# An audio tower on one core: chunks of the last stage staggered, softmax shares split into two single-pass products, softplus by chunk, means on GpSimd

## What is computed

```python
h = tok(x)                                   # patch embedding, layer norm
h = h + ssm(_layernorm(h), ...)              # 16 states per channel
h = h + moe(_layernorm(h), ...)              # 6 experts, one per token
h = h + _L1_attn_ref(_layernorm(h), ...)     # window of 7, 16 heads
h = h + _L1_ffn_ref(_layernorm(h), ...)      # 6 experts, all of them, weighted by sequence
```

```python
delta = jnp.minimum(jax.nn.softplus(x_ssm @ delta_W + delta_b), 0.5)
B_cont = 0.5 * (B_cont - jnp.mean(B_cont, axis=(0, 1), keepdims=True))
...
attn = jax.nn.softmax(attn, axis=-1)                    # 7 offsets x 16 heads
out = jnp.einsum('bhlk,bhlkd->bhld', attn, vg)
out = out.transpose(0, 2, 1, 3).reshape(B, L, C)
return out @ proj_w.T + proj_b
...
h = jax.nn.gelu(jnp.einsum('bsd,edf->ebsf', x, W1) + b1[:, None, None, :], approximate=False)
out_e = jnp.einsum('ebsf,efd->ebsd', h, W2) + b2[:, None, None, :]
return jnp.einsum('be,ebsd->bsd', expert_weights, out_e)
```

## Time and profile before

| | us |
|---|---|
| median of 3 runs | 953.21 |
| the runs | 950.11, 953.21, 1652.1 |
| the profiled execution, its own time | 950.27 |
| its span, first to last instruction | 948.3 |
| busy in the span: TensorE, VectorE, ScalarE, GpSimd | 643.1, 663.2, 487.5, 261.9 |
| mean granted TensorE clock | 0.835 |

### The profile page before, as it was taken

How to read it: one execution, slowest core, us unless ns; L and a number is a source line. 1 busy time by engine, 2 the same in 40 slices (tenths; PEclk the granted TensorE clock), 3 DMA queues, 4 the chain that set the end, 5 groups by cost and what they waited for, 6 DMA issues and landing times.

```text
span 948.3 us, 11034 instructions
## 1 busy us (share of the span) xinstructions
PE 643.1 (68%) x2992; PEld 473.6 (50%) x2993; DVE 663.2 (70%) x1458; ACT 487.5 (51%) x691; POOL 261.9 (28%) x266
## 2 busy tenths in 40 slices
PE   6984353745647527576650799357898898988986
PEld 3552253745546527553450477224555655655564
DVE  1977279999999999996862344266767677667651
ACT  1234699888989888831330233115353463443632
POOL 0443100000010001001487144231525426345242
PEclk9985677877768777698755799688999999999998
DMA  5300333553345434514211121200000000000000
GB/s 179 118 12 0 130 113 75 93 105 80 64 90 110 76 75 72 99 20 169 96 30 33 37 59 53 62 14 0 1 9 1 8 9 1 9 1 9 8 2 16
DMA packets 22519, 50.63 MB, mean 53 GB/s; under 512 B 4610, under 2 KB 14955, under 8 KB 22128
## 3 DMA queue, kind: packets, MB, share of 16 engines
q0 software_dynamic: 6752, 24.53, 13.2%
q1 hardware_dynamic: 15728, 25.64, 8.6%
HBM read 24.13 MB, written 10.10 MB: 36 GB/s over the span
## 4 chain that ended last, share of the span: by engine, by line
PE 39%; DVE 29%; issue 11%; ACT 10%; POOL 5%; POOLq 2%; DMA 2%; ACTq 1%; DVEq 0%; SPq 0%
PE psum L1715 5%; DVE s_R L1049 5%; DVE s_R L1059 5%; PE psum L1477 4%; DVE s_R L1054 4%; PE psum L1779 3%; PE psum L1644 3%; PE psum L1707 3%; PE psum L1657 2%; ACT s_R L879 2%; DVE s_R L1028 2%; POOLq L178 2%; POOL x_sorted L619 2%; DVE s_stat L203 2%; DVE s_xs L237 2%
## 5 line engine op out<-in xcount | busy, mean ns | idle before, releaser
L1538 PE MATMUL psum<-s_xn_lo,s_split_hi 128*128 128x368 f32 x256 | 101.3, 396 | 147.6 <-ACT s_R L783 99.2
L1538 PEld LDWEIGHTS psum<-s_xn_lo,s_split_hi 128*128 128x128 f32 x256 | 59.3, 232 | 153.2 <-ACT s_R L783 101.7
L1715 PE MATMUL psum<-s_R 128*128 128x368 f32 (+1 forms) x288 | 101.5, 473 | 0.0
L1054 DVE TENSOR_TENSOR_SCAN s_R<-s_R 128x2944 f32<-128x2944 f32 x16 | 100.7, 6291 | 0.6
L879 ACT ACTIVATE s_R<-psum,s_cols 128x368 f32<-128x368 f32 x96 | 52.2, 569 | 91.4 <-PE psum L1709 91.4
L1539 PE MATMUL psum<-s_xn_hi,s_split_lo 128*128 128x368 f32 x256 | 97.4, 381 | 0.0
L1540 PE MATMUL psum<-s_xn_hi,s_split_hi 128*128 128x368 f32 x256 | 96.6, 377 | 0.0
L604 POOL DMA_DIRECT2D s_xnfm<-s_R x14 | 17.1, 1219 | 271.2 <-DVEq L1063 271.2
L665 POOL TENSOR_TENSOR s_R<-s_R 128x368 f32<-128x368 f32 x48 | 45.4, 946 | 108.6 <-DVE s_R L1333 105.6
L1715 PEld LDWEIGHTS psum<-s_R 128*128 128x128 f32 (+1 forms) x288 | 53.0, 189 | 27.6
L1707 PE MATMUL psum<-s_xn_lo,s_split_hi 128*128 128x368 f32 x144 | 61.0, 424 | 7.1 <-ACT s_R L879 5.6
(11 more groups left out here) (219 smaller groups left out, 1506.0 us busy)
## 6 DMA issues: line engine op xcount, KB each, us to landing
s_xnfm<-s_R POOLq DMA_DIRECT2D x14, 1472.0 KB, 10.6
s_R<-in_xg SPq DMA_DIRECT2D x8, 744.0 KB, 4.2
x_sorted<-in_x_init SPq DMA_DIRECT2D x1, 5082.0 KB, 19.7
s_R<-in_w SPq DMA_DIRECT2D x2, 1536.0 KB, 9.5
s_wBC<-in_wBC SPq DMA_DIRECT2D x8, 256.0 KB, 2.9
s_R<-x_sorted SPq DMA_DIRECT2D x28, 66.0 KB, 1.8
s_R<-y_rows SPq DMA_DIRECT2D x8, 184.0 KB
out<-s_R SPq DMA_DIRECT2D x8, 184.0 KB
```

The costliest lines, as they stand in the source:

```text
L1054: dve.tensor_tensor_scan(bufB[:, u], ra[:, u], bufB[:, u], 0.0, ALU.mult, ALU.add).then_inc(ra_free, 1)
L1538: pe.matmul(bank(c), w_hi[:, s, u, k, :], xn_lo[:, a:b], start=True, stop=False)
L1715: ins = pe.matmul(bank((2, 4)[e % 2]), w, fh[0:kk, e % 3, j], start=(j == 0), stop=(j == FT - 1))
```

## The change

1. The barrier between stages 1 and 2 goes. ScalarE takes Exp and Ln per chunk, `softplus(i - 1)`, between `norm_second` and the copies of the next pair; a table set for both is asked for at the start; VectorE caps the argument instead of taking the minimum at the end. The first `wBC` is loaded with the first loads, and its split moves into stage 1. The first state's B and C go before the second state's Exp, Tanh and Exp.
2. The mean of B moves from VectorE (L1045, L1047) to GpSimd (`mean_of`, three small operations and a new wait of `drive`). GpSimd waits for the accumulation before it issues the next, not after. `weights_lo` goes ahead of `read_out`, and `read_out` no longer waits for itself.
3. Stage 5 has 10 turns. In turn `c`: attention of chunk `c`; projection, residual, norm and router of `c - 1`; the first 18 items of `FFN` for `c - 1`; the last 18 for `c - 2`. All four streams are reordered. One pair of items in `FFN` changes place.
4. The shares are split in `P_hi` (ScalarE, from PSUM) and `P_lo` (VectorE, PSUM less `P_hi`), and each offset's spread is two single-pass products instead of one fp32 product. `xn_hi`, `xn_lo` of the last stage hold two chunks only, which makes the room.

```diff
         def stage_end(eng, k):
             eng.drain().then_inc(stage_done, 1)
-            eng.wait_ge(stage_done, 4 * k)
+            eng.wait_ge(stage_done, 4 * (k - 1))
...
# list FFN
-               + [(1, 5, j) for j in range(FT)] + [(2, e, j) for e in (4, 5) for j in range(FT)])
+               + [(1, 5, 0), (1, 5, 1)] + [(2, 4, j) for j in range(FT)] + [(1, 5, 2)]
+               + [(2, 5, j) for j in range(FT)])
...
# GpSimd, stage 2
-            stage_end(pool, 1)
+            pool.wait_ge(x_split, NCH)
+            pool.wait_ge(delta_mm, NCH)
...
+            def add_state(n, u, first=False):
+                wait_apart(pool, prod_ready, n + 3)
+                if not first:
+                    wait_apart(pool, Y_added, 16 * n)
                 pool.dma_start(Y[:, :], bufC[:, u], accum_op=ALU.add, max_dma_last_dim=TOK // 2 * 4)\
                     .then_inc(Y_added, 16)
-                pool.wait_ge(Y_added, 16 * n + 16)
+            def mean_of(n, u):
+                wait_apart(pool, bc_free, NH + (n * 2 + 1) * NH)
+                wait_apart(pool, th_free, n + 1)
+                step.add(pool.tensor_tensor(part[:, u, 0:2], part[:, u, 0:2], part[:, u, 2:4], ALU.add))
+                step.wait()
+                step.add(pool.tensor_tensor(mean[:, u:u + 1], part[:, u, 0:1], part[:, u, 1:2], ALU.add))
+                step.wait(True)
+                pool.tensor_scalar(mean[:, u:u + 1], mean[:, u:u + 1], 1.0 / TOK, 0.0, ALU.mult, ALU.add)\
+                    .then_inc(mean_ready, 1)
+            mean_of(0, 0)
+            mean_of(1, 1)
+            add_state(0, 0, True)
+            add_state(1, 1)
+            for i in step.loop(NPAIR - 2, 2 * 2):
+                for u in range(2):
+                    mean_of(i * 2 + 2 + u, u)
+                for u in range(2):
+                    add_state(i * 2 + 2 + u, u)
+            mean_of(NS - 2, 0)
+            mean_of(NS - 1, 1)
...
# ScalarE, stages 1 and 2
+            act.preload_act_table_set("natural_log_exp_and_others")
...
+            def softplus(i):
+                for u in range(2):
+                    c = i * 2 + u
+                    d = dl[:, 1 + c * CT:1 + c * CT + CT]
+                    act.wait_ge(delta_read, 2 + c + 1)
+                    act.activation(d, d, ACT.Exp).then_inc(delta_act, 1)
+                    act.wait_ge(delta_act, 2 * c + 1)
+                    act.activation(d, d, ACT.Ln, bias=1.0, scale=1.0).then_inc(delta_act, 1)
+            bias_copy(0)
+            weights_hi(0, 0)
+            for i in range(NP):
+                if i + 1 < NP:
+                    bias_copy(i + 1)
+                normed_twice(i)
+                if i:
+                    softplus(i - 1)
+                norms_fm(i)
+            softplus(NP - 1)
+            load_table(ACT.Tanh, 0)
+            tanh(0, 0)
+            exp_minus(0)
+            exp_plus(0, 0)
+            silus(0, (0,), True)
+            exp_plus(1, 1)
+            tanh(1, 1)
+            exp_minus(1)
             weights_hi(1, 1)
+            silus(0, (1,), True)
...
# VectorE, stage 2
             def drive(n, u):
-                dve.wait_ge(bc_free, NH + (n * 2 + 1) * NH)
-                step.add(dve.reduce_sum(mean[:, u:u + 1], part[:, u, :], axis=AX))
-                step.wait()
-                step.add(dve.tensor_scalar(mean[:, u:u + 1], mean[:, u:u + 1], 1.0 / TOK, None, ALU.mult))
-                step.wait()
+                dve.wait_ge(ea_free, n + 2)
+                dve.wait_ge(mean_ready, n + 1)
...
# ScalarE, VectorE and TensorE, stage 5
+                act.activation(P_hi[:, c % 2], bank(3, OH), ACT.Copy).then_inc(P_hi_ready, 1)
+                dve.tensor_tensor(P_lo[:, c % 2], bank(3, OH), P_hi[:, c % 2].bitcast(f32), ALU.subtract)\
+                    .then_inc(P_fm_ready, 1)
-                        pe.matmul(bank(6 + o % 2), spread[:, o, :], P_fm[:, u], start=True, stop=True).then_inc(pb_mm, 1)
+                pe.matmul(bank(6 + o % 2), spread_r[:, o, :], P_lo[:, c % 2], start=True, stop=False)
+                pe.matmul(bank(6 + o % 2), spread_r[:, o, :], P_hi[:, c % 2], start=False, stop=True).then_inc(pb_mm, 1)
```

More of the change, by code:

```diff
@@ new lines, in _ @@
+            step.add(pool.memset(euler, math.e))
+            step.wait()
+            rstd_e(0)
+            for c in range(NCH + 2):
+                add_expert(c - 3, 5)
+                if c + 1 < NCH:
+                    rstd_e(c + 1)
+                add_expert(c - 2, 0)
+                add_expert(c - 2, 1)
+                if 1 <= c <= NCH:
+                    rstd_f(c - 1)
+                add_expert(c - 2, 2)
+                add_expert(c - 2, 3)
+                if c < NCH:
+                    projection_bias(c)
+                add_expert(c - 2, 4)
+                if c < NCH:
+                    weighted_sum(c, lambda: second_share(c - 1) if c else None)
+                elif c == NCH:
+                    second_share(c - 1)
@@ L912, in act_chunk @@
[L912 to L924 removed]
+                gelus(c - 2, 18, 21)
@@ L1080, in pair @@
                     decay(n + 3, 1)
-            dve.sem_inc(w_split, 1)
-            weights_lo(0, 0)
             injection(0, 0)
             decay(0, 0)
+            drive(0, 0)
+            recur(0, 0)
+            read_out(0, 0)
             decay(1, 1)
             injection(1, 1)
-            pair(0, 1)
-            for i in step.loop(NPAIR // 2 - 1, 2 * (2 * 2 + 2 * 3)):
+            weights_lo(1, 1)
+            drive(1, 1)
+            recur(1, 1)
+            injection(2, 0)
+            decay(2, 0)
+            read_out(1, 1)
+            injection(3, 1)
+            decay(3, 1)
+            for i in step.loop(NPAIR // 2 - 1, 2 * 2 * 2):
                 pair(i * 2 + 1, 0)
@@ new lines, in offset @@
+            def offset(c, o):
+                dve.wait_ge(pb_mm, c * K + o + 1)
+                if o >= 3:
+                    dve.wait_ge(pv_add, c * (K - 1) + o - 2)
+                dst_t = pv[:, c % 2] if o == 0 else pv_t[:, o % 2]
+                for dst, a, b in windowed(c % 2, o, bank(6 + o % 2), 2, dst_t):
+                    ins = dve.tensor_tensor(dst, a, b, ALU.mult)
+                ins.then_inc(pb_free, 1)
+            first_experts(0)
+            normed_e(0)
+            for c in range(NCH + 2):
+                f, att = c - 1, c < NCH
+                tail = 0 <= f < NCH
+                if 0 <= f - 1:
+                    expert_weights(f - 1)
+                weigh_expert(f - 1, 0)
+                weigh_expert(f - 1, 1)
+                if c + 1 < NCH:
+                    first_experts(c + 1)
+                if att:
+                    score_products(c)
+                if c == 0:
@@ new lines, in _ @@
+                weigh_expert(f - 1, 3)
+                if tail:
+                    normed_f(f)
+                if att:
+                    shares(c)
+                if tail:
+                    split_stream(f)
+                if att:
+                    shares_rest(c)
+                if tail:
+                    stream_sums(f)
+                weigh_expert(f - 1, 4)
+                for o in range(K):
+                    if att:
+                        offset(c, o)
+                    if o == 1 and c + 1 < NCH:
+                        normed_e(c + 1)
+                    if o == 2 and tail:
+                        router_largest(f)
+                    if o == 3:
+                        weigh_expert(f - 1, 5)
+                    if o == 4 and tail:
+                        router_second(f)
+                    if o == 5 and tail:
+                        router_weights(f)
@@ L1524, in _, with states @@
             delta(NP - 1)
-            stage_end(pe, 1)
-            def states(i, s):
+            def states(i, s, first=False):
                 for u in range(2):
@@ new lines, in project, with quarter @@
+            def project(c):
+                if c + 1 < NCH:
+                    pe.wait_ge(qkv_ready, (c + 1) * 3 + 1)
+                else:
+                    pe.wait_ge(pb_free, NCH * K)
+                pe.wait_ge(pv_add, (c + 1) * (K - 1))
+                for j in range(CB):
+                    ins = pe.matmul(bank_tm(6)[:, j, :], pv[:, c % 2, j * L:(j + 1) * L], w_proj, start=True, stop=True)
+                ins.then_inc(proj_mm, 1)
+            def quarter(q):
+                return psum[32 * q:min(32 * q + 32, OH), 3, 0:CT]
```

677 lines of the change are left out of this document (323 added, 354 removed).

## The result

| | us |
|---|---|
| median after, 4 runs | 919.6 (917.96, 919.01, 920.19, 920.49) |
| median before, beside them | 952.86 (lowest 950.11) |
| ratio | 0.967, 95% interval 0.965 to 0.969 |
| the profiled execution, its own time | 919.01 |
| its span | 917.2 |

The kernel is 33 us faster, inside the range and on the forecast side. The forecast was 912; it came out 7.6 slower. Three executions lie far above the rest and count in no ratio: 1652.1 and 987.8 of the kernel before, and 2055.6 of one experiment.

What follows compares the result with a forecast made beforehand. VectorE bounds the scan loop; in the last stage no engine is full, TensorE nearest. Stage 2 gives 12.5 us and the last stage 26, together 38.5 off 950.3: 912, own range 898 to 924, wider range 886 to 934.

Steps and rivals of the forecast that it cites:

- start of the last stage: Stage 5 begins 12.5 us earlier, from both parts of stage 2 together.
- to the first expert product of chunk 7: Tail of the last stage, from the last sixth offset: 17.3 us, where it was 10.8.
- Between stages 1 and 2: First drive at 116.4 instead of 133.0, 16.6 us earlier; 10 of it taken as kept at state 4.
- The tables rival: Between stages 1 and 2, each chunk's Exp and Ln load tables, 10 us back: 922 in total; chance 0.08.
- The pairs: Pairs of states in stage 2: 0.5 us less a pair, over 5.5 pairs from state 4 on, 2.7.
- The ring: One last-stage turn's circle through TensorE and VectorE: 32.6 us, plus 2.2 of blocking, period 34.8.
- The blocking of 2.2: Last stage: VectorE loses 2.2 us a turn to four GpSimd sums, 0.8 before the scores, 0.9 the shares, 0.5 later offsets.
- Six turns at 34.8: 209: Last stage: six turns after the second take 34.8 us each, 209 in all.
- The spreads: Last stage: seven spreads as two single-pass products each instead of one fp32 product, 2.0 us less TensorE work a turn.
- Full cover: Rival: VectorE and GpSimd rarely meet, last-stage period 32, means cost nothing, the start keeps 12: 888 us; chance 0.22.
- Hand-overs: Rival: TensorE and VectorE wait in turn, last-stage period 37.5, tail 50.5, stage 2 gains 8: 934 us; chance 0.17.
- The stalled scan: Rival: in stage 2 drive waits for GpSimd's means, up to 4.1 us a state: 980 us, slower; chance 0.03.

Runs made afterwards that it cites:

- the kernel with the front alone: The kernel before with only the edits of stages 1 and 2: 935.5 us, ratio 0.983.
- their experiment: The changed kernel with the means back on VectorE, sum and scale inside drive: 920.1 us, ratio 0.967.
- the moved bias addition: The changed kernel with GpSimd's addition of the projection bias moved behind expert sum 4: 906.3 us, ratio 0.953.
- the new order: The changed kernel with the shares of c ahead of the norm of f, transposes and copies alike: 900.8 us, ratio 0.948.
- the kernel with the earlier norm: The changed kernel with VectorE's norm of chunk c + 1 behind offset 0 instead of offset 1: 910.2 us, ratio 0.957.
- the experiment: The changed kernel with one fp32 product per spread instead of two single-pass products, without P_lo: 926.2 us, ratio 0.973.
- two moves of lines: The changed kernel with the shares ahead of the norm of f and the norm of c + 1 behind offset 0: 897.3 us, ratio 0.943.
- the front of before: The kernel before with only the edits of the last stage: 937.2 us, ratio 0.984.
- both moves: The changed kernel with the bias addition behind expert sum 4 and the shares ahead of the norm of f: 901.6 us, ratio 0.949.

## Why the prediction was right, and where it was off

The sum was 922.2 - 12.5 = 909.7 of span, measured 917.2; the 7.5 between them, step by step:

| step | forecast | measured |
|---|---|---|
| start of the last stage, against 611.5 | 12.5 earlier | 13.4 earlier; 13.0 to 16.7 in the other profiles with the front's edits |
| end of its first turn (sixth offset read) | 622.9 | 621.7 |
| second turn, to the next sixth offset | 29 | 29.4 |
| six turns | 209, 34.8 each | 215.1, 35.9 each; four dips in them |
| to the first expert product of chunk 7 | 17.3 | 18.1 |
| from there to the end | 31.5 | 32.9 |

That the start of the last stage came within 0.9 of the forecast is luck: three misses cancel there, the late start, a term of the pairs that was too small, and 2.5 lost behind the pairs (all below).

*Between stages 1 and 2: right.* Forecast 116.4 for the first `drive`; 114.6 to 115.8 in the profiles of all kernels with these edits, 118.62 in the one with the late start. At state 4 the kernel with the front alone is 9.0 ahead (10 forecast). The tables rival fell: ScalarE's timeline of the changed kernel has no load between those at 0.72 and 103.36, so none between the small activations. The 0 taken for it had no row of the kernel before behind it, only the name that the edit asks for.

```profile
100.68 0.51 ACT L767 ACTIVATE s_R<-s_R 128x368 f32<-128x368 f32 x1 [0.72 <-DVE s_R L1049]
101.23 0.51 ACT L769 ACTIVATE s_R<-s_R 128x368 f32<-128x368 f32 x1
...
103.36 1.28 ACT L745 ACT_TABLE_LOAD   x1
```

*The pairs: mis-sized.* The term was 0.5 a pair, "over 5.5 pairs from state 4 on: 2.7". It is 38.34 less 36.88, 1.5 a pair; from 9.0 ahead at state 4 the kernel with the front alone gets to 16.6 ahead at the last state. I had counted 0.5 and 0.76 to 1.3 and taken most of it back for the blocking. The means are worth 0.3 (their experiment), so 1.2 comes from the other edits of stage 2. No run takes these apart; what the timelines show gone are VectorE's waits around `read_out` and `weights_lo` (0.33, 0.26 and 0.30 in the pair of the earlier trace rows), which I had put at 0.5. (The two terms of stage 2, 10 and 2.7, make 12.7, not the 12.5 used.) Of these 16.6 (397.87 against 414.46), 2.5 are lost again before the last stage; where, no run settles.

*The ring: right in its length.* Forecast 32.6 and 2.2 of blocking, 34.8; measured 34.9 wherever the clock is full. From the turn that begins at 728.8 on: transposes to scores' end 12.3 (forecast 11.9 + 0.8), to the first spread 11.1 (10.6 + 0.9), to the transposes 11.5 (10.1 + 0.5). So two parts came 0.4 short of the forecast and the third 0.9 over, of which 0.37 is the wait for an offset; that the sum is off by 0.1 only is partly luck. The blocking of 2.2 is not where I put it either. The products of q and k take 3.07 in both kernels, so the expert sums cost nothing there; the norm of f loses 1.65 instead of 0.9, since the bias addition, which I had left out, falls on it as well. That the blocking on the shares stands on the ring is shown by the moved bias addition (34.9 to 33.9) and by the new order (33.1).

*The failed step: "Six turns at 34.8: 209".* It priced none of the six at a lower clock, as the five turns before from 686.36 on had none. Six turns took 6.1 longer, and of the 7.5 missed this is most: the six have four dips, and the turns without one take 34.9. One turn, with 37.1, is even above the 37 at which the prediction calls itself wrong. My ring named the idle time ahead of the first spread ("with some 1.7 left idle"; it is 1.8 for the shares and 0.5 for `P_lo`), but not that the clock can fall behind it. It falls at this place in every full turn with a dip of every profile. The five kernels in which this wait is at most 0.5 from the third turn on have no dip until the last 8 us; all that have one wait 0.9 or longer for the shares. So, by these profiles, the wait is part of the cause, but not all of it: the kernel with the earlier norm keeps it and four of its turns have no dip, and the kernel before waits 1.02 at this place and has none. Waits of 1.81 and 0.49 stand ahead of the fall at 782.5, and the same two also stand in turns at 1.00. By what mechanism the clock falls no run shows.

*The spreads* were priced at 2.0 a turn by their work; the experiment gives 0.8 by whole executions and 1.2 by the profiles, with a change in the dips in it.

*The rivals.* Full cover (888) needed a ring of 32: two moves of lines come near it, 32.6 and 897, so the bound was sound and this order just does not reach it. (For it, I had put most of TensorE's 3.9 idle round the softmax; the longest of these waits, 1.25, is for GpSimd's last sum, and 1.02 is for the shares.) Hand-overs (934) had turns of 37.5; the only one near it, 37.1, has a dip, which is another mechanism. The stalled scan fell: the waits for the means are 0.7 a pair, not 2.3 a state.

What stays open: why a given turn dips while the next, with the same idle 1.8, does not. It does not look like chance: two kernels that differ in stage 2 alone have the same pattern (turns of 35.44, 36.45, 34.88, 37.16, and with the means moved 35.48, 36.47, 34.87, 37.16), and the pattern is another with the front of before (four turns with a dip, and the last at 1.00). But each kernel has one profile only, so whether its pattern repeats is not shown.

## What to carry to other kernels

When an order of work is computed from durations at the full clock, look at TensorE's longest wait in the new ring as well: it is paid a second time if products behind it run at the lower clock (1.6 or 2.3 a turn here). Here the kernel before, with 3.9 idle in a turn but no wait above 1.25, had no dip, and the shorter ring with one wait of 1.8 had some. Beside a chain that GpSimd's sums can block, put VectorE's most urgent instructions first and the blocked ones behind them (900.8 against 919.6 here); moving the sum only helps if it does not land on the next such instruction (with both moves TensorE waited 1.08 for an offset instead of 0.39). Moving small operations to GpSimd from a VectorE that never rests saves little, since each of them can wait for a whole long instruction (3.00 instead of 0.2; 0.3 gained a pair here, for 0.76 of work moved).

## What the runs showed of the hardware

- More work, less time: 12 transposes added a turn gave 913.3 instead of 919.6 (3.3 of it seen in the last stage), and products of constants in the first turns 894.5 instead of 897.3.
- The clock fell to half (0.51 from 782.5 to 789.5) in a loop in which TensorE was busy for 32 of 34.9 us: for 4 us or for 7, always behind the same wait, at a price of 1.6 or 2.3 a turn.
- Who came second waited. VectorE's seven products of q and k, back to back, take 3.07, and GpSimd's normalization beside them (L226 at 766.62, 0.19 in the median) takes 3.24; but between the four short instructions of VectorE's norm of f GpSimd's sum of 1.00 gets in, and the norm takes 1.75 instead of 1.08, and 2.73 with the bias addition of 1.26 beside it too.
- GpSimd's issue of the accumulating DMA (L610) takes 1.20 in the median (1.19 to 1.47), whether `drive` runs beside it (218.14) or `injection` (236.18), and lands after 10.5 (10.4 to 11.2). It is not held up as its arithmetic is (3.00 for 0.2).
